# Three PSUM banks for the expert products and an early first turn, in a two-layer mixture-of-experts kernel

## The reference

```
# layer 1
y   = x @ W1[adapter]                      # per batch, one of 16 adapters
out = y @ base_w.T + base_b                # 1024 x 1024
h   = y @ A.T                              # 64 ranks
p   = softmax(y @ router_w.T)              # 16 experts, the best two kept
out += sum over the two experts e of  0.5 * gate_e * (h @ B[e].T)
x   = x + out
```

## Time and profile before

| | |
|---|---|
| median of three runs | 1176.64 us (1174.54 to 1177.17) |
| the profiled execution | 1176.69 us, its span 1175.1 us (1.59 us lie outside of the span) |
| TensorE busy | 1107.4 us of the span (94%) |
| VectorE / ScalarE / GpSimd busy | 58% / 43% / 19% |
| mean granted clock of TensorE | 0.986 of full speed |

### The profile page before, as it was taken

How to read it: one execution, slowest core, us unless ns; L and a number is a source line. 1 busy time by engine, 2 the same in 40 slices (tenths; PEclk the granted TensorE clock), 3 DMA queues, 4 the chain that set the end, 5 groups by cost and what they waited for, 6 DMA issues and landing times.

```text
span 1175.1 us, 22333 instructions
## 1 busy us (share of the span) xinstructions
PE 1107.4 (94%) x5801; PEld 916.0 (78%) x5802; DVE 686.9 (58%) x1321; ACT 504.1 (43%) x1027; POOL 220.1 (19%) x354
## 2 busy tenths in 40 slices
PE   4899979999999899999999999999999999999998
PEld 4899968878778687878878888766666778888886
DVE  4788943563745637463555486634444366566666
ACT  1112213553745536463555552135444344444443
POOL 1111110110201102010111000154444132223210
PEclk9899979999999899999999999999999999999999
DMA  6489755493755739474666342269988899999995
GB/s 210 163 304 322 268 213 184 131 336 101 271 206 203 254 103 321 159 258 148 219 223 212 104 116 90 79 231 325 325 321 316 299 396 345 346 347 337 316 330 205
DMA packets 114925, 283.11 MB, mean 241 GB/s; under 512 B 17202, under 2 KB 22322, under 8 KB 112946
## 3 DMA queue, kind: packets, MB, share of 16 engines
q1 hardware_dynamic: 85232, 178.95, 43.1%
q0 software_dynamic: 29216, 102.91, 25.7%
q10 hardware_dynamic: 418, 0.53, 0.2%
HBM read 181.65 MB, written 100.70 MB: 240 GB/s over the span
## 4 chain that ended last, share of the span: by engine, by line
PE 72%; DVE 12%; issue 5%; DMA 4%; ACT 2%; SPq 1%; ACTq 1%; DVEq 1%; POOL 0%; POOLq 0%
PE psum L1435 16%; PE psum L1437 16%; PE psum L1436 16%; PE psum L1632 4%; PE psum L1633 3%; PE psum L1529 3%; PE psum L1521 2%; PE psum L1641 2%; DVE x1g L1042 2%; PE psum L1547 2%; PE psum L1549 2%; PE psum L1530 2%; DMA xp<-act_scratch 2%; PE psum L1445 1%; ACT w L819 1%
## 5 line engine op out<-in xcount | busy, mean ns | idle before, releaser
L1435 PE MATMUL psum<-base_hi,xp_hi 128*128 128x512 f32 x512 | 204.5, 399 | 4.5 <-issue 1.9
L1437 PE MATMUL psum<-base_hi,xp_lo 128*128 128x512 f32 x512 | 200.3, 391 | 0.0
L1436 PE MATMUL psum<-base_lo,xp_hi 128*128 128x512 f32 x512 | 200.1, 391 | 0.0
L1435 PE MATMUL psum<-w,xp_hi 128*128 128x512 f32 x448 | 182.7, 408 | 5.0 <-DVE xp_lo L1092 2.3
L1437 PE MATMUL psum<-w,xp_lo 128*128 128x512 f32 x448 | 177.7, 397 | 0.0
L1436 PE MATMUL psum<-w,xp_hi 128*128 128x512 f32 x448 | 177.3, 396 | 0.0
L1074 DVE TENSOR_TENSOR w<-raw,w 128x1024 fp32r<-128x1024 f32 x112 | 132.4, 1221 | 29.4 <-ACT w L756 23.5
L637 POOL DMA_DIRECT2D raw<-w1T x112 | 59.1, 528 | 442.4 <-DVE w L1074 417.2
L801 ACT ACTIVATE xp_hi<-xp 128x256 fp32r<-128x256 f32 x124 | 51.4, 417 | 186.3 <-PE psum L1437 153.1
L1174 DVE TENSOR_TENSOR xp_lo<-xp,xp_hi 128x256 fp32r<-128x256 f32 x124 | 51.9, 425 | 120.2 <-ACT xp_hi L801 94.0
L1435 PEld LDWEIGHTS psum<-base_hi,xp_hi 128*128 128x128 f32 x512 | 96.3, 188 | 29.2 <-DVE xp_lo L1174 4.1
(11 more groups left out here) (278 smaller groups left out, 1911.8 us busy)
## 6 DMA issues: line engine op xcount, KB each, us to landing
raw<-w1T POOLq DMA_DIRECT2D x120, 512.0 KB, 5.7
delta_scratch<-dl SPq DMA_DIRECT2D x80, 512.0 KB
xp<-act_scratch SPq DMA_DIRECT2D x74, 256.0 KB, 3.4
act_scratch<-yT SPq DMA_DIRECT2D x72, 256.0 KB, 2.2
act_scratch<-x1g SPq DMA_DIRECT2D x16, 1024.0 KB, 5.2
x1t<-act_scratch SPq DMA_DIRECT2D x64, 256.0 KB
out<-x1t SPq DMA_DIRECT2D x62, 256.0 KB
xg<-xT SPq DMA_DIRECT2D x15, 1024.0 KB, 8.5
```

What stands on the lines that cost most here:

```text
L1435: mm(out, a_hi, b_hi, start=start, stop=False, skip_group_check=True)
L1436: mm(out, a_hi, b_lo, start=False, stop=False, skip_group_check=True)
L1437: return mm(out, a_lo, b_hi, start=False, stop=stop, skip_group_check=True)
```

## The change

The four banks that are not the base product's are used in another way in the expert stage: the products go round banks 0, 1, 2 (product 2s + h in bank (2s + h) mod 3), and the turned rows always stand in bank 7. So a product waits for the copy of the product three back (the other half, thus the other engine's semaphore), not two back. The second pair's turn now has a wait for the low part of the pair before. The first turn is issued after part 13 of tile 7, two parts ahead of the stage, and its high and low part are made ahead of the last `y_high`/`y_low` of tile 8.

```diff
-        def hwT_ps(m):
-            return bank(2 + m % 2 * 5)[:, 0:2 * P].rearrange("p (a r) -> p a r", a=2)
+        hwT_ps = bank(7)[:, 0:2 * P].rearrange("p (a r) -> p a r", a=2)
+
+        def delta_ps(s, h):
+            return bank((2 * s + h) % 3)
...
             for t in range(2, FIRST + 1):
                 for q in range(4):
+                    if t == FIRST and q == 3:
+                        hw_high(0)
                     y_high(t, q)
...
-            hw_high(0)
...
-                act.activation(dl[s % DRING][:, 512:1024], bank(1), ACT.Copy).then_inc(dl_act, 1)
+                act.activation(dl[s % DRING][:, 512:1024], delta_ps(s, 1), ACT.Copy).then_inc(dl_act, 1)
...
             for q in range(4):
+                if q == 3:
+                    hw_low(0)
                 y_low(8, q)
-            hw_low(0)
...
-                dve.tensor_copy(dl[s % DRING][:, 0:512], bank(0)).then_inc(dl_dve, 1)
+                dve.tensor_copy(dl[s % DRING][:, 0:512], delta_ps(s, 0)).then_inc(dl_dve, 1)
...
             def turn_hw(m):
-                if m >= 2:
-                    pe.wait_ge(hwl_done, m - 1)
+                if m >= 1:
+                    pe.wait_ge(hwl_done, m)
...
                 for h in range(2):
-                    if s > 0:
-                        pe.wait_ge(dl_act if h else dl_dve, s)
+                    if 2 * s + h >= 3:
+                        pe.wait_ge(dl_dve if h else dl_act, s - 1 + h)
                     m = experts[:, bass.ds(e * D + h * 512, 512)]
-                    mm(bank(h), hwh[:, s // 2 % 2, s % 2, :], m, start=True, stop=False, skip_group_check=True)
-                    mm(bank(h), hwl[:, s // 2 % 2, s % 2, :], m, start=False, stop=True, skip_group_check=True
+                    mm(delta_ps(s, h), hwh[:, s // 2 % 2, s % 2, :], m, start=True, stop=False, skip_group_check=True)
+                    mm(delta_ps(s, h), hwl[:, s // 2 % 2, s % 2, :], m, start=False, stop=True, skip_group_check=True
                        ).then_inc(x_done, 1)
...
                     if t == FIRST - 2 and n % 2 == 1:
                         row_sums(n // 2)
+                    if t == FIRST - 1 and n == 13:
+                        turn_hw(0)
...
             pe.wait_ge(etab_ready, 1)
             pe.wait_ge(exp_lo_done, E1)
-            turn_hw(0)
             e = expert_of(0)
```

More of the change, by code:

```diff
@@ L824, in hw_high @@
                     act.wait_ge(x_done, 4 * m - 4)
-                act.activation(hwh[:, m % 2, :, :], hwT_ps(m), ACT.Copy).then_inc(hwh_done, 1)
+                act.activation(hwh[:, m % 2, :, :], hwT_ps, ACT.Copy).then_inc(hwh_done, 1)
             act.wait_ge(mm_done, total * KC)
@@ L1288, in hw_low @@
                 dve.wait_ge(hwh_done, m + 1)
-                tt(hwl[:, m % 2, :, :], hwT_ps(m), hwh[:, m % 2, :, :].bitcast(F32), ALU.subtract
+                tt(hwl[:, m % 2, :, :], hwT_ps, hwh[:, m % 2, :, :].bitcast(F32), ALU.subtract
                    ).then_inc(hwl_done, 1)
@@ L1619, in turn_hw @@
                     pe.wait_ge(hwn_in[s % HRING], 16 * (s // HRING) + 16)
-                    last = pe.transpose(hwT_ps(m)[:, a, :], hwn[s % HRING][:, 0:2 * R1], ident[:, :])
+                    last = pe.transpose(hwT_ps[:, a, :], hwn[s % HRING][:, 0:2 * R1], ident[:, :])
                 last.then_inc(hwT_done, 1)
```

## The result

| | before | changed |
|---|---|---|
| median (five runs each, same chip) | 1176.64 us (1174.54 to 1178.77) | 1165.98 us (1163.94 to 1168.96) |
| the profiled execution, its span | 1176.69 us, 1175.1 us | 1167.17 us, 1165.6 us |
| first expert product | 771.65 us | 768.14 us |
| from it to the last step's (79) first product | 154.60 us | 149.77 us |
| from there to the end of the span | 248.85 us | 247.69 us |

The ratio of changed to before is 0.9922, 95% interval 0.9900 to 0.9944: faster by 9.2 us (6.6 to 11.8) by this ratio, while the two medians lie 10.7 us apart. The forecast was 1164.5 us, between 1160.5 and 1170.5.

A forecast was written before the change was run, and what follows sets the result against it. TensorE was taken to pace the expert stage and the last one, with gaps at late weight loads. 13.7 + 2.2 - 1.2 - 2.5 = 12.2 us, from 1176.7 to 1164.5 us; range 1160.5 to 1170.5 for 8 in 10.

The forecast's parts named there:

- the sequencer: TensorE's register work behind the wait at half 1: base weights load late, 0.03 us a pair, 1.2 us lost (0 to 5).
- the first turn: At the expert stage's start: turning after part 13 brings the first product earlier, 2.2 us gained (1.8 to 2.4).
- The transfers: Expert stage loads and stores: after a tile's load stores land late and hold copies, 2.5 us lost (0 to 7).
- three banks, 39 pairs: Even steps' half 0 no longer waits for VectorE's copy: 0.35 us a pair, 13.7 us gained.
- the wait only changes its place: Rival, 8%: copy at half 1 or sequencer behind it late by 0.3 us a pair; 1173.5 us.
- The ring of four: Rival, 16%: stores into the four dl buffers pace the steps behind each load, 7 us lost, not 2.5; 1169 us.
- the rival of the clock: Rival, 2%: TensorE's granted clock leaves full speed in the stage, 2.7 us longer per such pair; ten give 1191.5 us.

The follow-up runs named there:

- e3: Changed kernel with the next expert's number read ahead of the products, not behind them: 1163.47 us, ratio 0.9895 to the kernel before.
- e4: Changed kernel with the expert fixed at s // 5, so no number is read from the table: 1158.08 us, ratio 0.9861 to the kernel before.
- e8: Changed kernel with the read ahead of the products and the first turn after part 9, not 13: 1158.59 us, ratio 0.9866 to the kernel before.
- e11: Changed kernel with a ring of three dl buffers in place of four: 1171.91 us over ten runs, ratio 0.9973 to the kernel before.
- e10: e8 with a ring of six dl buffers in place of four: 1160.08 us, ratio 0.9877 to the kernel before.
- e2: Kernel before, still with two banks for the products, plus the early first turn alone: 1174.39 us, ratio 0.9989.
- e9: Changed kernel with only the first turn moved from part 13 to part 9 of tile 7: 1167.80 us, ratio 0.9931 to the kernel before.
- e1: Changed kernel with the first turn back where it was, so the three banks alone: 1167.86 us, ratio 0.9922 to the kernel before.
- e6: Kernel before, two banks, with the next expert's number read ahead of the products: 1171.69 us, ratio 0.9978.
- e7: Changed kernel with the read ahead of the products and the first turn back at the stage's start: 1162.04 us, ratio 0.9894 to the kernel before.
- e12: e8 unchanged, measured once more: 1159.35 us, ratio 0.9851 to the kernel before.
- e5: Changed kernel with half of each dl store's bytes in the expert stage, the other rows filled earlier: one run, 1196.65 us, only the stage read.

## Why the prediction was right, and where it wasn't

The time and the mechanism were right; two terms of the sum, the sequencer and the first turn, were mis-sized. The transfers, set too high, gave part of that back, and the spread of the runs did the rest. The terms, in the order of the prediction:

| term | predicted | measured |
|---|---|---|
| three banks, 39 pairs | +13.7 (0.35 each) | +13.2 (0.34 each, e3 against before) |
| sequencer | -1.2 (0 to -5) | -6.0 (39 x 0.16 = 6.3, changed against e3, less the transfers' 0.3 in it) |
| transfers | -2.5 (0 to -7) | about -0.3 |
| first turn | +2.2 | +2.2 at the first product, -1.7 in steps 0 to 3 |

**Three banks.** Right in mechanism and size: the late loads at half 0 are gone, and with the read out of the way the pair is 3.50 us.

**The sequencer is the step that failed.** The prediction saw that the read now stands behind the wait at half 1 and costed the rest of the sequencer's work at 0.75 us, with the 299 ns of the earlier trace rows in it. In step 34 of the changed kernel the read takes 555 ns, 0.26 us more. This step in the prediction's own terms: T is 831.73, VectorE's copy ended at T + 1.86 as forecast, and the base part's weights loaded at T + 2.91, where T + 2.70 had been forecast and T + 2.67 would still have been free. That makes a loss of 0.24 us by the prediction's own reckoning, and 0.24 was measured: the first matmul 0.14 late, the second 0.10 more. With a read of 303 ns, in step 42, the load stands at T + 2.66 (T is 847.24) and nothing is lost. The hold shows in the sequencer's rows of step 34: its work for half 1 is at 833.6, T + 1.9, where the forecast had it held until about T + 1.95. So the hold and the 0.75 us were right for a short read, and the length of the read is what was mis-sized: put into the same reckoning, the reads of the even steps give 0.13 us a pair in the mean, against 0.16 measured. The upper bound of 5 us was too low as well: it asked what a later hold would cost, and never what a longer read would. A duration taken where the read was short went unchanged into a kernel in which it isn't. The rival "the wait only changes its place" named the mechanism; its price, 0.3 us a pair, was twice what was measured.

**Transfers.** The ring of four cost nearly nothing: eight copies waited for stores, 7.8 us in all, and TensorE lost about 0.3 us by it, in step 40, where the second half's product came late. (Step 54, 2.36 us long, has copies held by stores as well, but its four products are on pace and its read takes 924 ns: that loss is the sequencer's.) The likely reason is the other error: with pairs of 3.66 us and not 3.5 the stores had time. The ring binds once the read is gone (e4, e8), and has little in hand even before (e11).

In the kernels with three banks and the read ahead the transfers run near their full share: 120 us of the stage of e3 have a share of 0.97 at 355 GB/s (windows, columns as in the earlier trace rows), e10 has 0.97 at 363, and only short stretches stand above, like that of 389 in the earlier trace rows. Even so the upper bound of 7 us is not borne out: e8 lost about 1.1 us in steps 39 and 55, e4 about 2.6 us in its three long ones.

```profile
780.00:900.00 120.00, 119.40 (x543) 94.03 (x542) 64.30 (x119) 64.13 (x127) 60.42 (x65) 1.00 0.97 355
```

**The first turn.** Its own chain ran as written: the transposes at 766.53, the low part at 767.36, the first product 0.24 us behind the last base matmul. The timeline of the changed kernel then shows the loss:

```profile
767.90 0.40 PE L1441 MATMUL psum<-base_hi,xp_lo 128*128 128x512 f32 x1
768.14 0.39 PE L1636 MATMUL psum<-w,hwh 128*128 x1
...
768.67 0.42 ACT L803 ACTIVATE xp_hi<-xp 128x256 fp32r<-128x256 f32 x1 [1.34 <-issue]
...
768.99 1.07 ACT L812 ACTIVATE held<-psum 128x512 f32<-128x512 f32 x2
...
770.10 0.69 DVE L1338 COPY dl<-psum 128x512 f32<-128x512 f32 x1 [0.55 <-issue]
...
770.93 0.50 PE L1636 MATMUL psum<-w,hwh 128*128 x1 [0.30 <-DVE dl L1338]
...
771.52 0.60 ACT L855 ACTIVATE dl<-psum 128x512 f32<-128x512 f32 x1 [1.46 <-PE psum L1637]
```

VectorE copied the first product at 770.10, 1.7 us behind its last matmul (768.37), and ScalarE its own only at 771.52, though it had been idle for 1.46 us. In step 34 above the same copies start 0.43 us behind the matmul. In e3 it is plainer, since ScalarE, idle for 3.57 us, has only this one release to wait for there:

```profile
764.70 0.40 PE L1441 MATMUL psum<-base_hi,xp_lo 128*128 128x512 f32 x1
...
767.69 0.42 ACT L803 ACTIVATE xp_hi<-xp 128x256 fp32r<-128x256 f32 x1 [3.57 <-remote]
```

The quarter `y_high(8, 3)` is released by the part whose last matmul is recorded at 764.70, and starts 2.99 us later; in e8 the same takes 0.43 us (767.78 to 768.21). Late first copies of this kind show in the changed kernel, e2, e3, e4, e9, e10 and e11, which have the early turn, and not in the four kernels with the late one (before, e1, e6, e7), whose TensorE stands still ahead of the stage in any case. But e8 and e12 have the early turn, too, and are free of it, and so is e5, with the turn after part 13 as in the changed kernel: its quarter starts 0.43 us behind the matmul.

```profile
790.39 0.40 PE L1446 MATMUL psum<-base_hi,xp_lo 128*128 128x512 f32 x1
...
790.82 0.42 ACT L808 ACTIVATE xp_hi<-xp 128x256 fp32r<-128x256 f32 x1 [1.01 <-PE psum L1446]
```

So it comes with the early turn and needs something more, which is neither the banks (e2 has two) nor the place of the turn (e9, e10 and, the other way, e5). Chance is unlikely after e12, but not excluded. What it is stays open.

**Why 1166 all the same.** The sum with the measured terms is 13.2 - 6.0 - 0.3 + 0.5 = 7.4 us, and the two profiles agree: 2.2 us at the first product, less 1.7 in steps 0 to 3, and 6.5 in steps 4 to 78 (146.9 against 140.4) make 7.0. Their spans differ by 9.5, as 1.3 us lie ahead of the turn, where the change does nothing, and 1.2 in the last stage. That part varies from one profile to the next without a system, 246.6 us in e6 and 250.3 in e3. The gain by the ratio is 9.2 us with an interval of 6.6 to 11.8, which holds the 7.0; the medians lie 10.7 apart. So the 12.2 us of the forecast were too many, and that the median came out 1.5 us from the forecast is in part luck: it is the runs' spread that brings it there.

**The clock** stood at 1.00 from 780 to 900 us in every kernel but e5 (0.96). Three banks in turn did not move it, so the rival of the clock finds no support here. Where it fell, at the stage's start, TensorE had stood idle before, as told below.

## What to carry to other kernels

Ask of every wait that is moved what the issuing engine's own sequencer does behind it: once the wait is the last thing to end, a register read placed after it costs what it takes beyond the slack (nothing at 303 ns here, 0.24 us at 555), and ahead of the wait the reads of e3, 597 ns in the middle, cost next to nothing outside of the long steps. Take the duration of such a read from its range over the trace (295 to 1214 ns here) and not from its median or one instance, and ask what the sum would be at either end: the change itself moved the median, for a reason that these runs don't show. And when two profiles are compared, compare the changed stage by its own first and last start: here the untouched rest varied by 3.7 us, about half of the 7.0 that the change gave.

## What the runs showed of the hardware

**The same read of a register by TensorE's sequencer took between 295 and 1545 ns, and the mean traffic doesn't tell when it is long.** Middle values of the 80 reads: 302 ns before, 307 ns in e6, 568 in the changed kernel, 597 in e3, 622 in e8; the longest, in e12, took 1545 ns. But e6 and the changed kernel have almost the same traffic (transfer share 0.92 at 329 GB/s and 0.93 at 335 GB/s over 780 to 900 us), and e5 with 214 GB/s there has 516 ns. Reads behind a tile's load are among the longest: in step 36 of the changed kernel, one of 1113 ns and the next of 939. What sets their length stays open.

**The clock fell after a short idle time, in some profiles.** In e1 TensorE was idle for 2.2 us before the first product, and some 1.4 us later its clock fell, to 0.50 of full speed from 774 to 776 us; matmuls then start 0.43 us apart (773.94 to 774.37), where the earlier trace rows have 0.42. Before, an idle time of 2.1 us at the same place left it at full (1.00 in every 2 us from 764 to 780). It fell in the same way in e2 (0.53 from 770 to 772 us), e3 (0.50 from 770 to 772) and e7 (0.51 from 772 to 774), and not in e4, e9, e10 and e11 (1.00 from 764 to 780), whose TensorE also waited in steps 1 and 2. From the start of one matmul to that of the next, the longest wait there was 2.04 to 2.45 us in the four kernels whose clock fell and 1.12 to 1.89 in these; but before and e6 had 2.36 and 2.37 without a fall, so the length alone doesn't decide it. The timeline of e1:

```profile
772.36 0.50 PE L1634 MATMUL psum<-w,hwh 128*128 x1 [2.18 <-DVE hwl L1291]
...
773.62 0.53 PE L1438 MATMUL psum<-base_lo,xp_hi 128*128 128x512 f32 x1
773.94 0.63 PE L1439 MATMUL psum<-base_hi,xp_lo 128*128 128x512 f32 x1
...
774.37 0.63 PE L1622 MATMUL psum<-ident,hwn 128*128 128x128 f32 x2
```

**Held weights cost a matmul 0.10 us** on top of the wait itself: where a matmul starts together with a load that was awaited, the next one starts 0.33 us after it (834.65 to 834.98 in the changed kernel), not 0.23. A load that is late by less costs nothing: in step 42 it starts 0.12 us late, 0.11 us ahead of its matmul, which is on pace.
